# Graph network on one Trainium2 core: a full stop of GpSimd at every eighth indirect transfer

## What is computed

```
support = xn @ weight                                    # layer 0
x += segment_sum(support[dst] * edge_weight, src) + bias + linear_attention0(xn)
x += shared_expert(xn) + sum of the top 2 of 8 private experts
messages = h_fwd[src] * direction[:, 0] + h_rev[src] * direction[:, 1]     # layer 1
out = per head: segment_sum(messages * softmax over the edges of a node, dst)
x += out + linear_attention1(xn)
agg = segment_sum(h[src] * alpha, dst)    # router: 32,768 edges and one loop a node
x += sum of the top 2 of 4 experts, chosen by layernorm(agg)
```

## Time and profile before

| | us |
|---|---|
| median of 3 runs | 2922.21 (2922.2 to 2924.8) |
| span of the profiled execution | 4223.8 |
| POOL busy in it | 2236.3 |
| PE, DVE, ACT busy in it | 2387.8, 1680.7, 1177.6 |
| L840, record scatters, busy | 754.5 (782 transfers) |
| L2373, messages' gather, busy | 443.8 (440 transfers) |
| L2947, attention's gather, busy | 242.0 (256 transfers) |

### The profile page before, as it was taken

The page is one execution under the profiler, slowest core; times in us unless marked ns, Lnnn a source line. Parts: engine busy times, 40 slices in busy tenths (PEclk is TensorE's granted clock), DMA queues, the critical chain, the costliest instruction groups (busy, mean ns, idle before and its releaser), DMA issues. The chain is left out here.

```text
span 4223.8 us, 36587 instructions
## 1 busy us (share of the span) xinstructions
PE 2387.8 (57%) x9996; PEld 1783.9 (42%) x9997; DVE 1680.7 (40%) x4678; ACT 1177.6 (28%) x3151; POOL 2236.3 (53%) x4104
## 2 busy tenths in 40 slices
PE   0034245445555536443259999736776675677784
PEld 0021134323443335112148887624455454455563
DVE  6510049955577731000000001435777674212225
ACT  0000013534444411000012221235785452222232
POOL 5777740057777755777730001367677735445441
PEclk9985555567777756555579999867997785778787
DMA  1000000043333312000036664122222231010101
GB/s 45 2 18 14 14 3 3 1 178 89 91 88 89 87 32 84 2 2 2 2 106 195 195 190 155 56 73 47 44 46 46 48 21 38 8 21 14 21 13 33
DMA packets 173406, 233.47 MB, mean 55 GB/s; under 512 B 59819, under 2 KB 136622, under 8 KB 172206
## 3 DMA queue, kind: packets, MB, share of 16 engines
q0 software_dynamic: 73664, 103.00, 11.2%
q1 hardware_dynamic: 96888, 118.21, 8.9%
q10 hardware_dynamic: 2678, 10.29, 0.6%
HBM read 192.31 MB, written 39.04 MB: 55 GB/s over the span
## 5 line engine op out<-in xcount | busy, mean ns | idle before, releaser
L840 POOL DMA_INDIRECT slots_gnn<-rec_gnn,slot_row_gnn x782 | 754.5, 965 | 299.6 <-issue 237.7
L1232 POOL DMA_INDIRECT rows_gnn<-support,xT x416 | 402.0, 966 | 437.1 <-DMA xT<-slots_gnn 276.9
L2373 POOL DMA_INDIRECT arena<-table,rec_gnn x440 | 443.8, 1009 | 195.2 <-issue 90.8
L2947 POOL DMA_INDIRECT source_rows<-table_g,source_router x256 | 242.0, 945 | 252.5 <-DVE weighted_rows L3191 158.9
L1277 PE MATMUL banks<-rows_gnn,one_hot 128*128 128x256 f32 x832 | 267.9, 483 | 184.1 <-issue 161.9
L3071 PE MATMUL banks<-xT,w 128*128 128x256 f32 (+1 forms) x832 | 232.0, 411 | 159.3 <-issue 148.2
L1721 POOL DMA_INDIRECT expert_row_ring<-slot_y,slot_from x50 | 48.0, 961 | 510.7 <-SPq L1822 457.3
L1277 PEld LDWEIGHTS banks<-rows_gnn,one_hot 128*128 128x128 f32 x832 | 197.2, 248 | 247.0 <-issue 205.6
L2472 PE MATMUL banks<-weighted,one_hot 128*128 128x260 f32 x880 | 273.4, 464 | 37.9 <-issue 22.1
L3071 PEld LDWEIGHTS banks<-xT,w 128*128 128x128 f32 x832 | 169.2, 209 | 210.6 <-issue 178.8
L1843 PE MATMUL banks<-slot_xT,w_private 128*128 128x256 f32 x1024 | 229.6, 383 | 33.5 <-ACT hidden_private L1885 31.5
(11 more groups left out here) (562 smaller groups left out, 4667.0 us busy)
## 6 DMA issues: line engine op xcount, KB each, us to landing
w_private<-in_w1p SPq DMA_DIRECT2D x32, 1024.0 KB
w_private<-in_w2p SPq DMA_DIRECT2D x32, 1024.0 KB
slots_gnn<-rec_gnn,slot_row_gnn POOLq DMA_INDIRECT x782
slot_x<-zero_rows ACTq DMA_DIRECT2D x8, 1024.0 KB
slot_rows<-slot_x SPq DMA_DIRECT2D x32, 256.0 KB
slot_y<-slot_out SPq DMA_DIRECT2D x32, 256.0 KB, 2.2
arena<-table,rec_gnn POOLq DMA_INDIRECT x440
rows_gnn<-support,xT POOLq DMA_INDIRECT x416
```

What stands on the lines that cost most here:

```text
L840: pool.indirect_dma_start(e.slots, bass.IndirectOffsetOnAxis(e.rows[:, j:j + 1], 0), e.rec[:, j, :], None)\
L1232: pool.indirect_dma_start(e.rows_in[:, k, :], None, table, bass.IndirectOffsetOnAxis(row, 0))\
L2373: pool.indirect_dma_start(c.raw[:, t % RAW_RING, :], None, c.table1, bass.IndirectOffsetOnAxis(row, 0))\
L2947: pool.indirect_dma_start(rows[:, k % 2, j - lo, :], None, c.table_g, bass.IndirectOffsetOnAxis(er.idx[:, j:j + 1], 0)).then_inc(rows_in[h ...
```

## The change

In the three loops POOL now waits before every eighth transfer until all transfers so far have landed. The four semaphores of the scatter and of the attention's gather become one each; the messages' gather keeps its four, since `sum1_stage` waits on them, and POOL waits for the halves issued since its last stop. The ring's wait for `summed1` stays where it was. No instruction moves on any engine: waits move, and DVE's four waits for a chunk of the attention become one.

```
+BURST = 8
...
@@ scatter_records
-    moved = [c.sem(ctx, f"records_moved_{e.name}_{begin}_{h}") for h in range(PARTS_IN_FLIGHT)]
+    moved = c.sem(ctx, f"records_moved_{e.name}_{begin}")
...
-            if turn and (j - begin) % HALF == 0:
-                pool.wait_ge(moved[h], 16 * HALF * turn)
+            if j > begin and (j - begin) % BURST == 0:
+                pool.wait_ge(moved, 16 * (j - begin))
                 pool.sem_inc(turns, 1)
...
-        for h in range(PARTS_IN_FLIGHT):
-            pool.wait_ge(moved[h], 16 * sum((j - begin) % FLIGHT // HALF == h for j in range(begin, end)))
+        pool.wait_ge(moved, 16 * (end - begin))
@@ gather_messages
-            h, turn = t % FLIGHT // HALF, t // FLIGHT
-            if t % HALF == 0 and turn:
-                pool.wait_ge(c.rows_in1[h], 16 * HALF * turn)
+            h = t % FLIGHT // HALF
+            if t % BURST == 0:
+                for before in range(max(t - BURST, 0) // HALF, t // HALF):
+                    pool.wait_ge(c.rows_in1[before % PARTS_IN_FLIGHT], 16 * HALF * (before // PARTS_IN_FLIGHT + 1))
+                    pool.sem_inc(turns, 1)
+            if t % HALF == 0 and t >= RAW_RING:
+                pool.wait_ge(c.summed1, (t - RAW_RING) // HALF + 1)
                 pool.sem_inc(turns, 1)
-                if t >= RAW_RING:
-                    pool.wait_ge(c.summed1, (t - RAW_RING) // HALF + 1)
-                    pool.sem_inc(turns, 1)
@@ attend_stage, gather
-                h, turn = j % FLIGHT // HALF, j // FLIGHT
-                if j % HALF == 0 and turn:
-                    pool.wait_ge(rows_in[h], 16 * HALF * turn)
+                if j and j % BURST == 0:
+                    pool.wait_ge(rows_in, 16 * j)
                     pool.sem_inc(turns, 1)
@@ attend_stage, DVE's chunk
-            for h in range(PARTS_IN_FLIGHT):
-                dve.wait_ge(rows_in[h], 16 * sum(j % FLIGHT // HALF == h for j in range(hi)))
+            dve.wait_ge(rows_in, 16 * hi)
```

More of the change, by code:

```diff
@@ L832, in _ @@
         for j in range(begin, end):
-            h, turn = (j - begin) % FLIGHT // HALF, (j - begin) // FLIGHT
             if j in e.heads:
@@ L836, in _ @@
                 pool.sem_inc(turns, 1)
-            if turn and (j - begin) % HALF == 0:
-                pool.wait_ge(moved[h], 16 * HALF * turn)
+            if j > begin and (j - begin) % BURST == 0:
+                pool.wait_ge(moved, 16 * (j - begin))
                 pool.sem_inc(turns, 1)
             pool.indirect_dma_start(e.slots, bass.IndirectOffsetOnAxis(e.rows[:, j:j + 1], 0), e.rec[:, j, :], None)\
-                .then_inc(moved[h], 16)
+                .then_inc(moved, 16)
             breathe(c, pool)
-        for h in range(PARTS_IN_FLIGHT):
-            pool.wait_ge(moved[h], 16 * sum((j - begin) % FLIGHT // HALF == h for j in range(begin, end)))
+        pool.wait_ge(moved, 16 * (end - begin))
 def tile_pairs():
@@ L2901, in attend_stage @@
     marks_in, turns = (c.sem(ctx, f"attend_{k}") for k in ("marks_in", "turns"))
-    rows_in = [c.sem(ctx, f"source_rows_in_{h}") for h in range(PARTS_IN_FLIGHT)]
+    rows_in = c.sem(ctx, "source_rows_in")
+    assert all(cut % BURST == 0 for cut in SLOT_CUTS)
     taken = c.sem(ctx, "source_rows_taken")
@@ L2942, in _ @@
             for j in range(lo, hi):
-                h, turn = j % FLIGHT // HALF, j // FLIGHT
-                if j % HALF == 0 and turn:
-                    pool.wait_ge(rows_in[h], 16 * HALF * turn)
+                if j and j % BURST == 0:
+                    pool.wait_ge(rows_in, 16 * j)
                     pool.sem_inc(turns, 1)
                 pool.indirect_dma_start(rows[:, k % 2, j - lo, :], None, c.table_g,
-                                        bass.IndirectOffsetOnAxis(er.idx[:, j:j + 1], 0)).then_inc(rows_in[h], 16)
+                                        bass.IndirectOffsetOnAxis(er.idx[:, j:j + 1], 0)).then_inc(rows_in, 16)
                 breathe(c, pool)
```

## The result

| | median us | range | runs |
|---|---|---|---|
| before, on the same chip | 2923.51 | 2922.2 to 2926.62 | 4 |
| changed | 3339.39 | 3337.43 to 3351.01 | 4 |

The ratio is 1.1426, with a 95% interval of [1.1408, 1.1444]: 416 us slower. The sign was forecast, the size was not: 2947 us was the figure and 3000 us the upper end.

The account below looks back on a forecast made before the run. No engine was taken as the bound throughout; with stops POOL would pace only the messages' gather. Terms 0 + 0 + 0 + 24.7 us on 2922.2 gave 2947 us, range 2915 to 3000.

Parts of the forecast that it names:

- As the trace stands, POOL is nowhere the bound: Whole kernel: in the profile read, POOL always ends ahead of or waits for others, 276.9 and 457.3 us after the scatters.
- the five stalls: Start of the messages' gather: PE, DVE and ACT stand together, 68.5 us in all, held to be absent from timed runs.
- Layer 0's scatter, "still hidden; cost 0": 48 stops, 65.3 us (95 at 1.98 each), hidden under a cover of 276.9 us, reckoned down to 109 us.
- Layer 1's scatter, "Hidden; cost 0": First 5 stops, 6.8 us, under a 41.1 us wait; other 42, 57 us, under a cover of 93 us.
- The attention's gather, cost 0: Two stops inside each chunk, 2.7 us, covered by 13.9 us at the last chunk; a chunk's first falls in DVE's wait.
- The messages' gather, +24.7 us: 54 stops lengthen POOL's path to 683.6 us against its readers' 658.9; bounds of the term 0 and 73.4 us.
- The readers' path of 658.9 us: Messages' gather: time of the engines reading the rows, 727.4 us as recorded, less 68.5 us of stalls.
- The price of one stop, 1.36 us: Each stop's addition at POOL, taken from ACT's start 1.67 us after the eighth messages transfer's issue, less 0.31.
- The other bound, 1.98 us: Addition per stop from an existing stop: POOL's gap of 2.17 us in place of 0.19 after the last 1 KB rows.
- A scatter shows too: Rival, chance 0.07: one scatter's stops come out of cover in full on top of the messages' term, 3012 us.
- The rival of a pause that lets others run freely: Rival, chance 0.09: under layer 0's scatter PE runs free during stops, 86 us less, 2836 us.
- All hidden: Rival, chance 0.26: timed runs have the cover that the trace shows, so nothing moves, 2922 us.

Follow-up runs that it names:

- the first recording: The profile of the kernel before that the prediction read, nothing edited; its span was 4223.8 us, 1301.6 us over the median of 2922.21 us.
- the second recording: The kernel before, unchanged, recorded once more after the result; it took 2924.76 us and its span was 2923.0 us.

## Why the prediction was wrong

**The reading of what bounds the kernel failed.** "As the trace stands, POOL is nowhere the bound" was true of the first recording and of no other: in the second POOL is busy in eight tenths of nearly every slice, and in the runs 180 stops cost 416 us. The prediction saw that its span was 1301.6 us too long, and named the five stalls and the slow PE, but took out 68.5 us of stalls in one stage and scaled two covers. It kept all other lengths as they stood. 1301.6 us had to come out somewhere; 276.9 - 6.3 = 270.6 of it came out of the wait at L1232, 409 of the one at L1721, and 158.7 us of the waits for DVE at L2947.

**Layer 0's scatter, "still hidden; cost 0"**, failed at the cover: 109 us were reckoned, and the wait at L1232 is 6.3 us with or without the stops, since the load of `xT` is behind the scatter's last record whatever comes before. The first gather starts at 655.5 us where it started at 559.3: 96 us for 48 stops, at the very end of the range of 65 to 95 us that had been put beside the 0.

**Layer 1's scatter, "Hidden; cost 0"**, failed by size: of the 93 us of cover 48.3 were there (55 with the waits that follow it), and the 47 stops of the layer, the first five included, cost (260.2 - 96.2) / 47 = 3.5 us each, the three long gaps that are no stops included, in place of 1.36. The 41.1 us that were to hide the first five are in no later recording either.

**The attention's gather, cost 0**, failed at the cover of 13.9 us and the wait for DVE, which is 0.2 us in the second recording. All 31 stops showed, 72.8 us.

**The messages' gather, +24.7 us**, measured 138.6. That POOL's path with the stops is longer than the readers' was right, but the term was mis-sized twice. The readers' path of 658.9 us was too long: in the second recording POOL issues from 1817.3 to 2407.2 us, 589.9 us, waits for the ring 0.6 us in all and is already the pace, so that each stop shows in full. That was the term's upper bound, 73.4 us. POOL's own path had been worked out well, 595.6 us; it was the readers' that held too much of the slowed recording, of which only the five longest stalls had been taken out. And the price was 2.5 us and not 1.36.

**The price of one stop, 1.36 us**, failed because it was read from the wrong engine: ACT's start after a landing holds nothing of the 0.7 us that POOL needs to start its next transfer. The other bound, 1.98 us, was POOL's own and was nearer. With it and no cover but L1721's, the sum would have been 180 x 1.98 - 55 = 301 us.

**The rivals.** "A scatter shows too", 3012 us at a chance of 0.07, was the nearest to the measured 3339, and covers turned out thin at every place and not at one. Neither it nor the forecast's range came near. The rival of a pause that lets others run freely did not come about: two stretches of the second recording, each under a scatter, answer to the earlier trace rows:

```profile
300.00:400.00 100.00, 64.18 (x758) 51.62 (x759) 90.66 (x158) 42.80 (x114) 86.13 (x151) 0.50 0.03 4
1300.00:1400.00 100.00, 100.00 (x479) 88.06 (x478) 9.68 (x14) 23.51 (x56) 85.19 (x159) 1.00 0.68 195
```

Where 73 matmuls stood in 100 us there are 758, and beside the private experts PE is busy throughout: there is nothing to free. "All hidden" rested on the first recording alone. The Trainium skill's 6.2 us between a profile's total and the time (Runtime: NRT & Kernel Launch, The ~15µs preamble/postamble breakdown) would put the profile over the time. The span of the second recording, from its first instruction to its last, is 1.8 us under its run's time, and the first one's is 1301.6 us over the median; neither is 6.2.

**Of what was to be seen in the new profile** the gap at the stops before L2373 was forecast near 1.7 us and is 2.2 to 6.3; the wait on L2472 for the ring was to go, and the nine that bear its name are stops, so it is gone, but it was next to nothing before, 0.6 us; the wait at L1232 was to shrink and did not; ACT's waits for rows at L2421 are many, as forecast, 55, but they were 29 in the second recording already.

## What to carry to other kernels

Before a sum is made on a recording, compare its span with the timed runs; if they lie far apart, record again, since no single correction of it gives back who waits for whom. Where one engine's queue of transfers is busy throughout, a wait is free only as long as enough transfers remain under way to span a landing: here two in a quiet stretch, while beside heavy loads even four left 12 us of waiting at 42 stops, which other waits hid; a full drain cost 416 / 180 = 2.3 us of the run in the mean. Read the price of a stop from the engine that stops, not from another that waits for the same event.

## What the runs showed that was not expected

POOL restarts 0.7 to 0.8 us after another engine has seen the same landing. A memset between two indirect transfers costs nothing here: the step is 1.27 us with it and without. 194 GB/s of traffic in place of 66, from loads on another queue, raise a drain by about 1 us. A single recording of a kernel can be 1.44 times as long as its runs, with PE, DVE and ACT standing still together in it.
